# The first two tiles' expert products at the end of the causal stage, in shared PSUM banks

## Chip, cores and metric

One core of a Trainium2 chip. The metric is the device time in microseconds (us) of one execution of the whole program, the median over several runs; lower is better. The profile shows one execution, taken by the hardware profiler. Its engines: PE is TensorE's matmuls and PEld its weight loads, DVE is VectorE, ACT ScalarE, POOL GpSimd, SP SyncE; a name with a q (PEq) is the engine's instruction sequencer.

## The reference

Four residual blocks on x of shape (8, 512, 128), each `x = x + layernorm(block(layernorm(x)))`: a dilated attention, a ternary-weight linear layer, a 16-head attention with a gate, and a last block made of a causal grouped-query attention and a mixture of experts. Only the last one is touched:

```python
h = x + _gqa(_rmsnorm(x, attn_norm_w), wq, wk, wv, wo)     # causal, 16 heads of 8, 4 KV heads
out = h + _moe(_rmsnorm(h, ffn_norm_w), gate_w, expert_w)
# _moe, t: (tokens, 128)
logits = t @ gate_w.T                                      # 8 experts
w, sel = jax.lax.top_k(logits, 2)
w = jax.nn.softmax(w, axis=1)
comb = jnp.sum(w[..., None] * jax.nn.one_hot(sel, 8), axis=1)
for e in range(8):
    out = out + comb[:, e, None] * (t @ expert_w[e].T)
```

All eight experts' products are computed for every token, and weighted with `comb`, which is zero for six of them.

## The kernel before

The 4096 tokens are 32 tiles of 128 tokens, in four chunks of eight tiles (`TILES`, `CT`, `CHUNKS`). The program has five stages, one function each; every stage is a block in which each engine runs its own list of instructions, ordered against the others by semaphores alone. A stage ends with a barrier: each engine drains, GpSimd collects their signals and releases them, clears the stage's semaphores (`Phase.close`, line 55), and a second collect-and-release follows (recorded at lines 57 and 58).

**The causal stage** (`causal_attention_phase`, line 1287) works batch by batch in turns of three units for each pair of heads. TensorE makes transposed scores into `pT`, two PSUM buffers of two banks each (line 1320, used in turn); ScalarE takes their exponential into `P` and counts the semaphore `P` up (line 1566), 24 (`NT`) for each of the 8 (`B`) batches; GpSimd masks them (1446); TensorE multiplies them with the values into `pO` (1628) and transposes the result back to tokens (`by_token`, 1640, matmuls at 1643); ScalarE takes it out (`take`, 1546), VectorE inverts the sums (1482), GpSimd divides (1415). Score rings `pS` fill three further banks, `pO` the last one. After the last batch's scores nine more turns (`LAST_TURNS`) finish what is left of the outputs; their last TensorE work is the `by_token` of the last group.

In the last batch's turns, chunks 0 and 1 (`EARLY` = 2) of the mixture of experts are prepared as well (`early_turn`): attention by channel (transposes), projection, residual, h by channel, mean square, gate logits, the choice of two experts (`choose`, 1213) and the weights `comb` (`weigh`, 1238). So at the stage's end, `h` by channel of chunk 0 (`top.oT[0]`), and `comb` of chunks 0 and 1 are there.

**The experts stage** (`experts_phase`, line 1692) goes over turns u = 0 to 41, written out in each engine's list. In turn u:

- TensorE multiplies tile u's tokens (128 columns of `hT`) with all eight experts' weights, two matmuls of 512 columns in fp32 into `PE_[u % 3]`, a ring of three buffers of two banks each (lines 1943 to 1950). From tile 3 on it waits until VectorE has finished tile u - 3 (`scaled_d`). Each of these fp32 matmuls is two records in the profile, so a tile is four.
- ScalarE scales experts 0 to 3 out of PSUM into `T` (1907), once the product is there (`exp_psum`), and then VectorE adds experts 4 to 7, four fused multiply-adds (`scale_tile`, 1800 to 1808).
- GpSimd adds the four partial sums (1778, 1781).

The same lists hold the preparation of chunks 2 and 3, one step at a time, in the turns that `HEAD_AT` and the step tables set (lines 1724 to 1728): `HEAD_AT` is the turn of a chunk's first step, and each table gives the distance to it. TensorE's steps are the transposes into `PA` (recorded at line 1266), the projection (1275), the transposes of h (1266) and the gate (1282), at distances 0, 3, 6 and 9; VectorE's are residual (3), choose (8) and weigh (11); ScalarE's the copy (0), mean square (4), copy (6) and exponential (10). In a turn the tile comes first and the steps follow. The sum with h and the layernorm go by groups of four tiles: `total` of group g in turn 5 + 4g and `scalars` in turn 9 + 4g on VectorE, `normalise` in turn 11 + 4g on ScalarE, `finish` on GpSimd, and a store for each group.

Of the kernel before, what the change touches and what calls it, by code (L numbers as in the profile page):

```python
# [11 lines left out]
B, S, D = 8, 512, 128  # L12
R = 4
SEG = 64
TILES = B * R
CT = 8
# [6 lines left out]
HD4, KV4, NE = 8, 4, 8  # L23
# [1260 lines left out]
    last.then_inc(top.moe["logits"], 1)  # L1284


def causal_attention_phase(nc, top, dram):


# [9 lines left out]
    with ExitStack() as ctx:  # L1299
        ph = Phase(nc, ctx, "d_")  # L1300
        sm = ph.sems("part1 rest1 part2 rest2 parts mT_psum mT ST P masked PV O_sb O_T O_raw rden O_tok half_power")
        two = range(2)
        RING = 3
# [10 lines left out]
        P = [ph.sb(f"P{k}", [128, 2, PAIRW]) for k in range(4)]  # L1314
        OT = [ph.sb(f"OT{k}", [128, S]) for k in two]
        Or = [ph.sb(f"Or{k}", [128, QT, 2, 4, HD4 + 1]) for k in two]
        rden = [ph.sb(f"rden{k}", [128, QT, 2, 4]) for k in two]
        ring = ph.ps("pS", [128, RING, 512])
        pS = [ring[:, k, :] for k in range(RING)]
        pT = [ph.ps(f"pT{k}", [128, 2, 512]) for k in two]  # L1320
        pO = ph.ps("pO", [128, S])
        pM = [pT[ROWS_UNIT % 2][0:3 * HEADS, j, S - 128:S].bitcast(BF16) for j in two]

        NS, NT, NG = 3 * HEADS, 3 * HEADS // 2, KV4
# [56 lines left out]
        with nc.Block() as block:  # L1381
# [208 lines left out]
            def _(pe):  # L1590
# [75 lines left out]
                def early_turn(u):  # L1666
                    for step, k in early_steps(u, PE_STEPS):
                        if step == "attention_by_channel":
                            pe.wait_ge(S_max, B * NS)
                            pe.wait_ge(sm["O_tok"], 2 * (NG // 2) * (k + 1))  # L1670
                            wait(pe, early["hT"], k)
                            tokens_by_channel(nc, top, PA, O4[k]).then_inc(early["oT_psum"], 1)
                        if step == "project":
                            project(nc, pe, top, PA, k)
                        if step == "h_by_channel":
                            pe.wait_ge(early["h"], k + 1)
                            tokens_by_channel(nc, top, PA, h[k]).then_inc(early["hT_psum"], 1)
                        if step == "gate":
                            wait(pe, early["scale"], k)
                            gate(nc, pe, top, logits, k)  # L1680
# [5 lines left out]
                for pair, unit in LAST_TURNS:  # L1686
                    outputs(B, B // 2, 0, pair, unit)
                    early_turn(3 * HEADS // 2 + 3 * pair + unit)
        ph.close()


def experts_phase(nc, top, dram, out):
# [5 lines left out]
    with ExitStack() as ctx:  # L1698
        ph = Phase(nc, ctx, "e_")
# [3 lines left out]
        two = range(2)  # L1703
# [6 lines left out]
        st, mv = small("st", CT, 6), small("mv", CT, 2)  # L1710
        PART = NE // 2
        T = [ph.sb(f"T{k}", [128, PART, D]) for k in range(4)]
        PA = ph.ps("PA", [128, CT, D])
        RING = 3
        PE_ = [ph.ps(f"PE{k}", [128, NE, D]) for k in range(RING)]
        HALF = CT // 2
        GROUPS = TILES // HALF
        LAST = GROUPS - 1
# [2 lines left out]
        h = [top.N4[:, CT * c:CT * c + CT, :] for c in chunks]  # L1721
        O4 = [top.O4[:, CT * c:CT * c + CT, :] for c in chunks]

        HEAD_AT = {2: 1, 3: 12}
        PE_STEPS = {0: "attention_by_channel", 3: "project", 6: "h_by_channel", 9: "gate"}
        DVE_STEPS = {3: "residual", 8: "choose", 11: "weigh"}
        ACT_STEPS = {0: "attention_by_channel", 4: "mean_square", 6: "h_by_channel", 10: "exp_difference"}
# [13 lines left out]
        with nc.Block() as block:  # L1741
# [125 lines left out]
            @block.scalar  # L1867
            def _(act):
                def attention_by_channel(c):
                    act.wait_ge(early["oT_psum"], c + 1)  # L1870
                    nc.scalar.activation(oT[c][:, :, :], by_batch(PA[:, :, :]), ACT.Copy).then_inc(early["oT"], 1)

                def h_by_channel(c):
                    act.wait_ge(early["hT_psum"], c + 1)
                    nc.scalar.activation(hT[c][:, :, :], by_batch(PA[:, :, :]), ACT.Copy).then_inc(early["hT"], 1)

                def mean_square(c):
                    act.wait_ge(early["h"], c + 1)
                    for t in range(CT):

                        last = nc.scalar.activation(moe[c][:, t, :], h[c][:, t, :], ACT.Square,
                                                    accum_out=top.sq[c][:, t:t + 1])
                    last.then_inc(sm["sq"], 1)

                def deviation_last():

                    act.wait_ge(sm["mv"], LAST + 1)
                    nc.scalar.activation(by_group(std, LAST), by_group(mv, LAST)[:, :, 1], ACT.Sqrt, bias=top.eps[:, :])\
                        .then_inc(sm["dev"], 1)

                def normalise(g):
                    y, rstd, shift = by_group(h, g), by_group(rs, g), by_group(std, g)
                    act.wait_ge(sm["norm"], g + 1)
                    for t in range(2 if g == LAST else HALF):
                        last = nc.scalar.activation(y[:, t, :], y[:, t, :], ACT.Identity,
                                                    bias=shift[:, t:t + 1], scale=rstd[:, t:t + 1])
                    last.then_inc(sm["y"], 1)

                for u in TURNS:
                    if 0 <= u < TILES:  # L1900
                        act.wait_ge(early["comb"], u // CT + 1)
                        act.wait_ge(sm["exp_psum"], u + 1)
                        if u >= 4:

                            act.wait_ge(sm["summed"], u - 3)
                        for e in range(PART):
                            last = nc.scalar.activation(T[u % 4][:, e, :], PE_[u % RING][:, e, :], ACT.Copy,  # L1907
                                                        scale=comb[u // CT][:, u % CT, e:e + 1])
                        last.then_inc(sm["scaled_a"], 1)
                    for step, c in due(u, ACT_STEPS):  # L1910
                        if step == "attention_by_channel":
                            attention_by_channel(c)
                        if step == "h_by_channel":
                            h_by_channel(c)
                        if step == "mean_square":
                            mean_square(c)
                        if step == "exp_difference":
                            exp_difference(nc, act, top, c)
                            if c == CHUNKS - 1:
                                nc.scalar.activation(std[c][:, 0:1], top.eps[:, :], ACT.Sqrt)  # L1920
                    for g in group_due(u, "deviation"):
                        if g == LAST:
                            deviation_last()
                    for g in group_due(u, "normalise"):
                        normalise(g)

            @block.tensor
            def _(pe):
                def mm(out_, lhsT, rhs, start=True, stop=True):
                    return nc.tensor.matmul(out_, lhsT, rhs, start=start, stop=stop)  # L1930

                def attention_by_channel(c):
                    pe.wait_ge(early["scale"], c)
                    tokens_by_channel(nc, top, PA, O4[c]).then_inc(early["oT_psum"], 1)

                def h_by_channel(c):
                    pe.wait_ge(early["h"], c + 1)
                    tokens_by_channel(nc, top, PA, h[c]).then_inc(early["hT_psum"], 1)

                tokens = lambda c, t: hT[c][:, t // 4, 128 * (t % 4):128 * (t % 4) + 128]  # L1940

                for u in TURNS:
                    if 0 <= u < TILES:
                        if u >= RING:

                            pe.wait_ge(sm["scaled_d"], u - RING + 1)
                        for a in two:
                            last = mm(PE_[u % RING][:, 4 * a:4 * a + 4, :], tokens(u // CT, u % CT),
                                      top.gate_expT[:, NE + 512 * a:NE + 512 * a + 512])
                        last.then_inc(sm["exp_psum"], 1)  # L1950
                    for step, c in due(u, PE_STEPS):
                        if step == "attention_by_channel":
                            attention_by_channel(c)
                        if step == "project":
                            project(nc, pe, top, PA, c)
                        if step == "h_by_channel":
                            h_by_channel(c)
                        if step == "gate":
                            gate(nc, pe, top, PA[:, 0, :], c)
# [3 lines left out]
def sandwich(nc, dram, out):  # L1963
    with ExitStack() as ctx:
# [68 lines left out]
        dilated_and_ternary_phase(nc, top, dram)  # L2033
        gated_attention_phase(nc, top, dram)
        projection_phase(nc, top, dram)
        causal_attention_phase(nc, top, dram)
        experts_phase(nc, top, dram, out)


# [64 lines left out]
```

## Time and profile before

| | |
|---|---|
| median of 3 runs | 686.95 us (686.89 to 688.94) |
| profiled execution, its own time | 687.56 us |
| its span, first to last instruction | 685.8 us |
| mean granted TensorE clock | 0.84 of 2.4 GHz |
| busy: PE, DVE, ACT, POOL | 548.0, 506.5, 360.7, 268.0 us |
| causal stage's last work ends / experts stage's first matmul | 586.3 / 587.57 us after the span's start |

Times within the profile are counted from the span's start. An average busy share says little of one boundary between two stages; for this change the stretch from 584 us to the end of the span counts, and in it which wait ends last. The ends of matmuls are modelled, so the distance between starts tells more than a duration. A granted clock of 1.00 is 2.4 GHz, 0.50 is 1.2 GHz.

### The profile page before, as it was taken

Reading aid. Unit: us, or ns where it says so; the run is one execution under the profiler, and the core shown is the slowest. Engines: PE = TensorE matmul, PEld = TensorE weight load, DVE = VectorE, ACT = ScalarE, POOL = GpSimd, SP = SyncE. Lnnn points to the kernel's source line nnn. Section 1 sums busy time; section 2 is a strip of 40 time slices with the busy share of each in tenths; the row PEclk is TensorE's granted clock in tenths of the full one; section 3 lists DMA queues with packets and bytes.
Section 4 is the critical chain, followed back from the end, with each engine's and each line's share of the span. In section 5 each row is a group of like instructions: output and inputs, shape, how many; then the busy total and the mean of one; then the engine's idle time right before and its main releaser. Section 6 shows DMA issues by size and latency. Waiting matters only on the chain. (4 is left out here: it accounts for less than half of the span.)

```text
span 685.8 us, 11832 instructions
## 1 busy us (share of the span) xinstructions
PE 548.0 (80%) x3800; PEld 307.6 (45%) x3800; DVE 506.5 (74%) x2314; ACT 360.7 (53%) x738; POOL 268.0 (39%) x499
## 2 busy tenths in 40 slices
PE   1866478838967699867999999999999898798870
PEld 1856367727656466411233333333333454455420
DVE  6599999371273678688989999999997155269784
ACT  5841134500120467601478878878878754456762
POOL 2001007720002267810254544555455454266774
PEclk9996565555897699955599999999999998899996
DMA  8000000000000038510011211111210000000001
GB/s 315 1 1 1 0 1 1 0 1 0 1 1 1 0 119 227 169 62 6 1 36 32 63 31 35 34 33 37 58 36 1 7 1 1 2 0 16 32 16 61
DMA packets 17580, 24.77 MB, mean 36 GB/s; under 512 B 3246, under 2 KB 14014, under 8 KB 17342
## 3 DMA queue, kind: packets, MB, share of 16 engines
q1 hardware_dynamic: 16942, 21.91, 10.4%
q10 hardware_dynamic: 576, 2.10, 0.8%
q8 instruction: 30, 0.49, 0.3%
q14 instruction: 32, 0.26, 0.1%
HBM read 13.65 MB, written 10.35 MB: 35 GB/s over the span
## 5 line engine op out<-in xcount | busy, mean ns | idle before, releaser
L905 DVE CUSTOM_DVE_ANT_0 w_qkvT<-d_pS,w_qkvT 128x512 bf16<-128x512 f32 x480 | 203.9, 486 | 16.7 <-PE d_pS L896 11.8
L1566 ACT ACTIVATE d_P<-d_pT 128x768 f32<-128x768 f32 (+1 forms) x192 | 165.9, 882 | 62.7 <-PE d_pT L1592 61.1
L1446 POOL TENSOR_SCALAR_AFFINE_SELECT d_P<-d_P 128x256 f32<-128x256 f32 x256 | 102.6, 415 | 134.0 <-ACT d_P L1566 133.9
L896 PE MATMUL d_pS<-Ks,Qs 48*128 48x512 bf16 x480 | 97.8, 324 | 12.8 <-DVE hadamard L905 8.9
L1592 PE MATMUL d_pO<-d_P,V 128*32 128x512 f32 (+3 forms) x1024 | 98.5, 460 | 1.4 <-POOL d_P L1446 0.9
L1592 PE MATMUL d_pT<-Qs,Ks 51*128 51x512 bf16 (+3 forms) x512 | 72.9, 312 | 2.0 <-ACT d_mT L1536 2.0
L896 PEld LDWEIGHTS d_pS<-Ks,Qs 48*128 48x128 bf16 x480 | 32.2, 96 | 56.1 <-DVE hadamard L905 51.9
L1592 PEld LDWEIGHTS d_pT<-Qs,Ks 51*128 51x128 bf16 x512 | 20.7, 95 | 74.1 <-ACT d_P L1566 42.3
L1930 PE MATMUL e_PE<-gate_expT,w_qkvT 128*128 128x512 f32 x96 | 44.8, 614 | 6.3 <-DVE e_T L1804 3.5
L1804 DVE SCALAR_TENSOR_TENSOR e_T<-e_PE,comb,e_T 128x128 f32<-128x128 f32 x128 | 35.2, 343 | 19.2 <-ACT e_T L1907 19.2
L1907 ACT ACTIVATE e_T<-e_PE,comb 128x128 f32<-128x128 f32 x128 | 36.1, 377 | 24.8 <-issue 14.5
L905 DVE DVE_READ_ACCUMULATOR2_ANT hadamard<- 128x1 f32 x512 | 42.4, 83 | 0.0
L1592 PEld LDWEIGHTS d_pO<-d_P,V 128*32 128x32 f32 x1024 | 21.2, 110 | 32.6 <-issue 29.7
L1778 POOL TENSOR_TENSOR e_T<-e_T 128x256 f32<-128x256 f32 x32 | 24.4, 763 | 26.9 <-DVE e_T L1804 26.8
L453 POOL MEMSET a_expS<- 1x1024 f32 x4 | 3.8, 945 | 78.7 <-DVE a_q L263 78.7
L460 POOL TENSOR_SCALAR N<-X,a_mv_s,a_rs 128x128 f32<-128x128 f32 x32 | 25.1, 798 | 20.5 <-DVE a_rs L317 20.5
L1930 PEld LDWEIGHTS e_PE<-gate_expT,w_qkvT 128*128 128x128 f32 x96 | 18.0, 197 | 26.8 <-issue 21.1
L990 POOL MEMSET c_rms_bias<- 128x1 f32 x1 | 0.1, 98 | 76.3 <-POOLq L58 76.3
L978 POOL TENSOR_SCALAR N<-X,c_x_mv,c_rs 128x128 f32<-128x128 f32 x32 | 24.9, 783 | 7.3 <-DVE c_nb L1039 7.3
L1643 PE MATMUL d_pO<-ident,d_OT 128*128 128x128 f32 x128 | 21.7, 294 | 3.4 <-ACT d_OT L1554 3.1
L138 DVE BATCH_NORM_STATS2 a_st_s<-X 128x6 f32<-128x128 f32 x96 | 19.6, 278 | 6.1 <-DMA X<-in_x_dram 6.1
L368 ACT ACTIVATE a_nT<-a_PS 128x1024 f32<-128x1024 f32 x12 | 12.3, 1022 | 22.1 <-PE a_PS L476 22.0
(311 smaller groups left out, 1036.6 us busy)
## 6 DMA issues: line engine op xcount, KB each, us to landing
Qs<-q_stack SPq DMA_DIRECT2D x32, 192.0 KB, 3.1
q_stack<-Qp SPq DMA_DIRECT2D x8, 384.0 KB, 2.6
X<-in_x_dram ACTq DMA_DIRECT2D x4, 512.0 KB, 6.1
q_stack<-Qp SPq DMA_DIRECT2D x8, 256.0 KB, 2.5
out_dram<-e_moe SPq DMA_DIRECT2D x8, 256.0 KB, 2.0
w_qkvT<-in_w_qkvT_dram SPq DMA_DIRECT2D x1, 1536.0 KB
Ks<-k_stack SPq DMA_DIRECT2D x32, 48.0 KB, 3.2
q_stack<-Qp SPq DMA_DIRECT2D x8, 128.0 KB, 2.1
```

Source lines behind the costliest of these rows:

```text
L460: last = nc.gpsimd.tensor_scalar(n[c][:, t, :], X[c][:, t, :], mv["s3_"][c][:, t, 0:1], rs3[c][:, t:t + 1], ALU.subtract, ALU.mult)
L896: last = nc.tensor.matmul(dst[:, at:at + w], top.Qs[c][rows, h % 8, 128 * q:128 * q + 128], top.Ks[c][rows, h // 4 % 2, 0:w], start=True, ...
L905: last = nc.vector.tensor_tensor_reduce(out=junk[:, at:at + w], in0=src[:, at:at + w], in1=top.wide_mask[:, 512 - w:512], scale=1.0, scala ...
L978: last = nc.gpsimd.tensor_scalar(N4[:, R * n + t, :], X[:, R * n + t, :], x_mv[n][:, t, 0:1], rs[n][:, 0, t:t + 1], ALU.subtract, ALU.mult)
L1446: last = nc.gpsimd.affine_select(out=view, in_=view, compare_op=ALU.is_ge, fill=0.0, base=0, pattern=[[0, 2], [1, 128]], channel_multiplie ...
L1566: nc.scalar.activation(P[pair % 4][:, :, P_AT[unit]:P_AT[unit] + w], pT[(3 * pair + unit) % 2][:, :, 0:w], ACT.Exp, scale=float(HD4) ** -0 ...
L1592: return nc.tensor.matmul(out, lhsT, rhs, start=start, stop=stop)
L1643: last = nc.tensor.transpose(pO[:, 128 * q:128 * q + 128], OT[g % 2][:, 128 * q:128 * q + 128], top.ident[:, :])
L1778: nc.gpsimd.tensor_tensor(product[:, 0:2, :], product[:, 0:2, :], product[:, 2:4, :], ALU.add)\
L1804: last = nc.vector.scalar_tensor_tensor(out=T[u % 4][:, j, :], in0=PE_[u % RING][:, PART + j, :], scalar=comb[u // CT][:, u % CT, PART + j ...
L1907: last = nc.scalar.activation(T[u % 4][:, e, :], PE_[u % RING][:, e, :], ACT.Copy, scale=comb[u // CT][:, u % CT, e:e + 1])
L1930: return nc.tensor.matmul(out_, lhsT, rhs, start=start, stop=stop)
```

## The change

`pT` is taken from the causal stage and given to the top level, so that both stages hold the same four banks. At the very end of the causal stage's TensorE list, behind the last transposes, the products of tiles 0 and 1 are made into its two buffers. In the experts stage these are the first two buffers of the ring of three; TensorE starts with tile 2, ScalarE waits for no product in turns 0 and 1 (the barrier between the stages stands for it), and chunk 2's steps start in turn 2 instead of 1.

```diff
+EARLY_TILES = 2
+
+def expert_products(nc, top, dst, c, t):
+    tokens = top.oT[c][:, t // 4, 128 * (t % 4):128 * (t % 4) + 128]
+    for a in range(2):
+        last = nc.tensor.matmul(dst[:, a, :], tokens, top.gate_expT[:, NE + 512 * a:NE + 512 * a + 512], start=True, stop=True)
+    return last
...
 # causal_attention_phase
+        pT = top.pT
         ring = ph.ps("pS", [128, RING, 512])
         pS = [ring[:, k, :] for k in range(RING)]
-        pT = [ph.ps(f"pT{k}", [128, 2, 512]) for k in two]
...
                 for pair, unit in LAST_TURNS:
                     outputs(B, B // 2, 0, pair, unit)
                     early_turn(3 * HEADS // 2 + 3 * pair + unit)
+
+                pe.wait_ge(sm["P"], B * NT)
+                for t in range(EARLY_TILES):
+                    expert_products(nc, top, pT[t][:, :, :], 0, t)
         ph.close()
...
 # experts_phase
+        RING = 3
+        PE_ = [t[:, :, :].rearrange("p a (e d) -> p (a e) d", d=D) for t in (*top.pT, ph.ps("PE", [128, 2, 512]))]
         PA = ph.ps("PA", [128, CT, D])
-        RING = 3
-        PE_ = [ph.ps(f"PE{k}", [128, NE, D]) for k in range(RING)]
...
-        HEAD_AT = {2: 1, 3: 12}
+        HEAD_AT = {2: 2, 3: 12}
...
                         act.wait_ge(early["comb"], u // CT + 1)
-                        act.wait_ge(sm["exp_psum"], u + 1)
+                        if u >= EARLY_TILES:
+                            act.wait_ge(sm["exp_psum"], u - EARLY_TILES + 1)
...
-                    if 0 <= u < TILES:
+                    if EARLY_TILES <= u < TILES:
                         if u >= RING:
                             pe.wait_ge(sm["scaled_d"], u - RING + 1)
-                        for a in two:
-                            last = mm(PE_[u % RING][:, 4 * a:4 * a + 4, :], tokens(u // CT, u % CT),
-                                      top.gate_expT[:, NE + 512 * a:NE + 512 * a + 512])
-                        last.then_inc(sm["exp_psum"], 1)
+                        expert_products(nc, top, PE_[u % RING].rearrange("p (a e) d -> p a (e d)", a=2),
+                                        u // CT, u % CT).then_inc(sm["exp_psum"], 1)
...
 # sandwich
+        top.pT = [top.ps(f"pT{k}", [128, 2, 512]) for k in range(2)]
         causal_attention_phase(nc, top, dram)
```

## Rows read from the trace of the kernel before

**Rows 1.** The chain that ended last, in order of time: start us, us, what.

```profile
587.57 5.16 PE e_PE L1930 x8
592.73 0.87 PE e_PA L1266 x8
593.60 5.15 PE e_PE L1930 x12
598.75 3.61 PE e_PA L1275 x16
...
613.56 1.70 PE e_PA L1282 x16
...
630.50 4.39 PE e_PE L1930 x11
```

**Rows 2.** Timeline, causal stage's last work: start us, us, engine line op out<-in xcount.

```profile
584.12 0.66 PE L1643 MATMUL d_pO<-ident,d_OT 128*128 128x128 f32 x4 [0.71 <-ACT d_OT L1554]
584.81 0.36 ACT L1546 ACTIVATE d_Or<-d_pO 128x72 f32<-128x72 f32 x2 [0.75 <-PE d_pO L1643]
585.26 0.35 DVE L1482 RECIPROCAL d_rden<-d_Or 128x32 f32<-128x32 f32 x1 [4.59 <-ACT d_Or L1546]
585.70 0.63 POOL L1415 TENSOR_TENSOR O<-d_Or,d_rden 128x256 f32<-128x256 f32 x1 [6.95 <-DVE d_rden L1482]
```

**Rows 3.** Windows: length, busy us (x) PE PEld DVE ACT POOL, granted clock, DMA.

```profile
584.00:584.50 0.50, 0.38 (x3) 0.38 (x4) 0.00 (x0) 0.07 (x1) 0.00 (x0) 1.00 0.00 0
...
586.50:587.00 0.50, 0.00 (x0) 0.00 (x0) 0.00 (x0) 0.00 (x0) 0.00 (x0) 1.00 0.00 0
...
590.00:590.50 0.50, 0.50 (x2) 0.24 (x1) 0.00 (x0) 0.00 (x0) 0.00 (x0) 0.50 0.00 0
...
591.00:591.50 0.50, 0.50 (x3) 0.23 (x2) 0.00 (x0) 0.39 (x2) 0.00 (x0) 1.00 0.00 0
```

**Rows 4.** Semaphore events of the causal and projection stages' ends: ns, then start us.

```profile
L1381 PEldq DRAIN  x1: 700/700/700, 584.1 to 584.1; - x1
...
L1381 POOLq DRAIN  x1: 736/736/736, 585.7 to 585.7; - x1
...
L58 PEldq EVENT_SEMAPHORE  x1: 51/51/51, 587.5 to 587.5; - x1
...
L954 DVEq DRAIN  x1: 673/673/673, 304.3 to 304.3; - x1
...
L58 PEldq EVENT_SEMAPHORE  x1: 51/51/51, 305.7 to 305.7; - x1
```

**Rows 5.** Timeline, TensorE in the experts stage: behind tile 1, ahead of tile 13.

```profile
592.57 1.04 PE L1266 MATMUL e_PA<-ident,O 128*128 128x128 f32 x8
...
621.48 5.42 PE L1930 MATMUL e_PE<-gate_expT,w_qkvT 128*128 128x512 f32 x12 [1.82 <-DVE e_T L1804]
```

**Rows 6.** Timeline, ScalarE: tile 0, copy, tiles 5 and 6 (mean square between).

```profile
591.12 1.14 ACT L1907 ACTIVATE e_T<-e_PE,comb 128x128 f32<-128x128 f32 x4 [5.94 <-PE e_PE L1930]
...
593.85 1.04 ACT L1871 ACTIVATE w_qkvT<-e_PA 128x1024 f32<-128x1024 f32 x1
...
604.17 1.14 ACT L1907 ACTIVATE e_T<-e_PE,comb 128x128 f32<-128x128 f32 x4 [4.19 <-issue]
...
607.52 2.16 ACT L1907 ACTIVATE e_T<-e_PE,comb 128x128 f32<-128x128 f32 x8
```

**Rows 7.** Timeline, VectorE: choose, total, tiles 10 and 11, weigh, tile 13.

```profile
615.36 0.23 DVE L1218 TENSOR_TENSOR logit<-e_PA,rr 128x64 f32<-128x64 f32 x1 [1.13 <-PE e_PA L1282]
...
618.14 0.68 DVE L1813 TENSOR_TENSOR N<-N,e_moe 128x512 f32<-128x512 f32 x1
...
620.31 2.15 DVE L1804 SCALAR_TENSOR_TENSOR e_T<-e_PE,comb,e_T 128x128 f32<-128x128 f32 x8
...
624.16 0.16 DVE L1242 TENSOR_SCALAR weights<-weights 128x8 f32<-128x8 f32 x1
...
626.78 1.13 DVE L1804 SCALAR_TENSOR_TENSOR e_T<-e_PE,comb,e_T 128x128 f32<-128x128 f32 x4
```

## The prediction

> **What bounds the kernel now.** I read first the chain of waits, because only the stretch around the boundary between the causal and the experts stage is touched. It runs on TensorE from 587.57 us on: eight matmul records of the products of tiles 0 and 1 take 5.16 us, then transposes, products and projection follow back to back until the gate's matmuls, which start at 613.56 and take 1.70 [rows 1]. So from the stage's first instruction until about 615.3 TensorE sets the pace, and later the chain changes between VectorE, ScalarE and TensorE. The reader is to see there that one product tile is four records, 5.15 us for twelve, thus 1.72 us a tile at the steady rate, while the first two tiles took 592.57 - 587.57 = 5.0 us instead of 3.4 [rows 1, 5].
>
> Second, the timeline of the causal stage's last 3 us: TensorE's last four transposes start at 584.12 and follow each other so that it is free at about 584.8; ScalarE, VectorE and GpSimd then take the last group out (584.81, 585.26, 585.70) and TensorE has nothing until 587.57 [rows 2]. Third, the granted clock in half-microsecond windows: it is 1.00 (2.4 GHz) while those transposes run and still 1.00 at 586.5 to 587.0, where TensorE is idle; after that idle stretch it is 0.50 (1.2 GHz) under the first products, and 1.00 again from 591.0, after some 3 us of products [rows 3]. Fourth, the semaphore events of the stage's end: TensorE's drain ends at 584.8, GpSimd's at 585.7 + 0.74 = 586.4, and TensorE is released into the experts stage at 587.5, so 1.06 us behind the last drain; at the end of the projection stage the last drain (VectorE's) ended at 304.3 + 0.67 = 304.97 and the release came at 305.7, 0.73 us behind it [rows 4].
>
> **The edits, one by one.** *Products moved across the barrier.* Eight records leave the start of the experts stage (5.0 us there) and go behind the transposes. Their wait is for the last exponential, long past, so it costs nothing; nothing is queued behind them on TensorE but its drain, and the signal that ScalarE waits for comes ahead of them. They issue no DMA. They start at 584.8. If the clock stays at 2.4 GHz they take 8 x 0.43 = 3.44 us, to 588.2; if it falls for all of them, 8 x 0.86 = 6.86 us, to 591.6 (0.86 is twice 0.43, the clock being halved; before, low records followed by high ones made the 5.0). I take the first: the level was 1.00 at their start and stayed so until 587.0 with an idle engine [rows 3], and now the engine is busy in that stretch. As for the gap behind them (about 1 us), the clock stayed up through 1.82 us of idle ahead of tile 13, whose twelve records with their neighbours took 5.42 us as everywhere at the high rate [rows 5].
>
> The Trainium skill ("TensorE: Matmul & The Clock Gate", the part on the clock gate) says that the throttled clock is the default and that sustained activity releases it, which speaks against work put behind a thin stretch; by it the products could run at 1.2 GHz in part or in whole, and the sum would be that of the first rival.
>
> *The barrier.* It now waits for TensorE instead of GpSimd: it is the new wait that the change adds, and all four other engines stand behind it. 588.25, plus a handshake of between 0.73 and 1.06 (the two cases above [rows 4]); I take 0.85, because TensorE, like VectorE in the projection's end, comes last while GpSimd has long been drained. Release at 589.1, first matmul (tile 2) at 589.15, the 0.07 being that of before [rows 1, 4]. Before, TensorE had done tiles 0 and 1 at 592.57 and turned to the transposes [rows 5]. Gain at this point: 592.57 - 589.15 = 3.4 us.
>
> *ScalarE's missing waits.* Tiles 0 and 1 need no signal: ScalarE starts at 589.1 instead of 591.12 [rows 6], and VectorE one ScalarE tile later, at 590.3. Tile 3 reuses the first bank and needs VectorE's tile 0, done by about 591.4; TensorE comes to it at 591.74, so the ring of three has no new wait. The third ring buffer and the other banks change place, with no operation attached: nothing.
>
> *Chunk 2's steps one turn later.* Transposes, projection, h by channel and gate (0.87 + 3.61 + 0.87 + 1.70 = 7.05 us [rows 1]) keep their sizes. On TensorE ten tiles (2 to 11) now stand ahead of the gate's end instead of eleven: it ends at 589.15 + 10 x 1.717 + 7.05 = 613.4, where before it ended at 613.56 + 1.70 = 615.26. Then tile 12, the next transposes and tile 13 run to 613.4 + 1.72 + 0.87 + 1.72 = 617.7.
>
> What did VectorE make of it before? Between the gate and tile 10 it did choose (615.36 to 618.14), total and scalars (618.14 to 620.31), then tile 10, and TensorE sat idle for 1.82 us ahead of tile 13 [rows 5, 7]. After the change, total(1) and scalars(0) are still in turn 9 but choose is in turn 10, behind tile 10. ScalarE: tile 6's product ends at 602.2, tile and mean square take 607.52 - 604.17 = 3.35 us [rows 6], to 605.65; tiles 7 and 8 1.05 each, the copy 1.0 and tile 9 1.05: 609.8. VectorE: tile 9 until 610.95, total and scalars 2.25, tile 10 1.05, choose 2.8, tile 11 1.05: 618.1. Tile 14 needs that and starts at 618.15 instead of 617.7. The stall of 1.82 becomes 0.5, a gain of 1.3. Its bounds are a stall of nothing (gain 1.8) and the old one (gain 0).
>
> *What is late next.* VectorE, behind tile 13 (done at 620.2): weigh, at most 626.78 - 624.16 = 2.6, total and scalars 2.25, tile 14 1.05, makes 626.1. TensorE asks for tile 17 after tiles 14 to 16 and the projection, 618.15 + 5.15 + 3.61 = 626.9. So 0.8 us of cover are left. From turn 14 on both kernels do the same steps in the same order; the projection of chunk 3, tile 16 (630.50 before [rows 1]) and all that hangs on it come earlier by the whole gain.
>
> **The sum.** 3.4 + 1.3 = 4.7 us. The profiled execution took 687.56 us (span 685.8 and 1.76 around it): 682.9. The median of the runs, 686.95, is 0.6 below the profiled one, and this gives **682.3**.
>
> **The rivals.** *First, a low clock under the early products.* If the clock is down when they start and rises after some 3 us of them, as in the experts stage before [rows 3], they take 5.1 instead of 3.44 us, the gain is 1.7 smaller, 3.0: 684.0. For it: the level changes at moments that need not lie the same way to the work in every execution, and 3 us later, under the first products of before, it is down; against it: the transposes at 584.12 ran at 1.00. At the low level for all of them, the gain falls to 1.3: 685.7.
>
> *Second, the stall only moves.* If VectorE still makes TensorE wait 1.8 us around tiles 13 to 17, the start's 3.4 us is all: 683.6. For it: total, choose and weigh are as long as ever; against it: the cover worked out above.
>
> *Third, no difference.* VectorE's pile behind tile 13 exceeds its cover of 0.8 us by another 3 or more, so that most of the gain is returned at tile 17: about 685.5 to 686. For it: such VectorE operations stretch beside GpSimd ones (this weigh took 2.6 us); against it: it would have to double. The change does what it says, as far as the diff shows: the products do leave the stage.
>
> *Fourth, slower, by one mechanism: the clock stays low across the barrier.* All eight records at 0.86 put tile 2 at 584.8 + 6.86 + 0.9 = 592.56, and each further tile at the low level costs 1.72 more. With the 1.3 of the stall, two such tiles (low until 599.4) give 3.44 - 1.3 = +2.1 us, 689.1; from there on it is measurably slower. Against it: before, the clock came back by 591.0 after 3 us of just this work [rows 3].
>
> **How the numbers follow.** Forecast 0.58, first rival 0.17 (with its extreme), second 0.14, third 0.08, fourth 0.03. About 0.3%, 2.1 us, is what a measurement of this kernel can tell from no change. Faster by more: the forecast and the first two but for the extreme, 0.87; within: 0.10; slower: 0.03. The range takes in a full loss of the stall and the shorter handshake at its low end (4.7 + 0.5 + 0.1, and a little for the runs' own spread: 681.2) and both first rivals, to 685.2, at its high end; outside are the third and fourth and the first's extreme.
>
> **What would show it.** Right: eight product records from 584.8 to 588.2 (0.43 us apart) in the causal stage; the release 0.7 to 1.1 us behind TensorE's drain; ScalarE's tile 0 at about 589.1; the gate ending near 613.4; an idle of about 0.5 instead of 1.82 us ahead of tile 14 and little ahead of tile 13; tile 16 some 4.7 us earlier and the tail unchanged in length. Wrong: records 0.86 us apart (first or fourth rival); an idle of 1.5 us or more at tiles 13 to 17 released by VectorE (second, third); a release much later than 1.1 us behind the drain.

## The result and the profile after

The changed kernel took 683.59 us (median of 6 runs, 683.05 to 684.03), the kernel before 689.0 (6 runs, 686.89 to 690.23); the ratio of the two is 0.9925, with a 95% interval of 0.9908 to 0.9941. In a second comparison the ratio was 0.992 (0.9892 to 0.9948). That is 4 to 6 us faster in the first, around the 4.7 us that were forecast; 683.59 lies 1.3 us above the forecast 682.3 and within its range of 681.2 to 685.2. The three runs of the kernel before that were known at first, with a median of 686.95, were its quicker ones. All ratios here and below leave out two disturbed executions, one of 2357.49 us (of the version with one early tile) and one of 710.1 us (of the kernel before).

The profiled execution of the changed kernel took 683.05 us, its span is 681.3 us. TensorE's timeline of it, to be held against [rows 1, 2, 5]; columns are start us, us, engine, line, operation, tiles, shapes, count, idle before and releaser:

```profile
583.38 0.65 PE L1654 MATMUL d_pO<-ident,d_OT 128*128 128x128 f32 x4 [0.71 <-ACT d_OT L1565]
583.87 3.60 PE L1294 MATMUL pT<-gate_expT,w_qkvT 128*128 128x512 f32 x8
588.66 1.96 PE L1294 MATMUL e_PE<-gate_expT,w_qkvT 128*128 128x512 f32 x4 [1.19 <-PEq L58]
590.45 1.04 PE L1266 MATMUL e_PA<-ident,O 128*128 128x128 f32 x8
...
615.66 1.88 PE L1294 MATMUL pT<-gate_expT,w_qkvT 128*128 128x512 f32 x4
618.23 1.99 PE L1294 MATMUL e_PE<-gate_expT,w_qkvT 128*128 128x512 f32 x4 [0.69 <-DVE e_T L1819]
...
625.38 1.88 PE L1294 MATMUL pT<-gate_expT,w_qkvT 128*128 128x512 f32 x4
...
637.19 1.98 PE L1294 MATMUL pT<-gate_expT,w_qkvT 128*128 128x512 f32 x4 [1.68 <-DVE e_T L1819]
```

The rows are, from above: the last transposes of the causal stage, the eight early records, tile 2, the transposes of chunk 2, tile 13, tile 14, tile 16 and tile 21. The early products run right behind the transposes, 0.43 us apart, 3.6 us in all. Tile 2 starts at 588.66. The idle of 1.82 us ahead of tile 13 [rows 5] has gone, and tile 14 has one of 0.69.

The granted clock of the changed kernel, in windows as in [rows 3]:

```profile
584.50:585.00 0.50, 0.50 (x2) 0.19 (x1) 0.35 (x1) 0.00 (x0) 0.05 (x1) 1.00 0.00 0
...
588.00:588.50 0.50, 0.00 (x0) 0.00 (x0) 0.00 (x0) 0.00 (x0) 0.00 (x0) 1.00 0.00 0
...
589.50:590.00 0.50, 0.50 (x2) 0.19 (x1) 0.19 (x1) 0.50 (x4) 0.00 (x0) 1.00 0.05 16
```

It stays at 2.4 GHz through the products, the idle 1.19 us of the barrier, and the first tiles behind it, where the kernel before had 1.2 GHz.

The events of the stage's end, to be held against [rows 4]:

```profile
L1392 PEldq DRAIN  x1: 4053/4053/4053, 583.4 to 583.4; - x1
...
L1392 POOLq DRAIN  x1: 737/737/737, 584.9 to 584.9; - x1
...
L58 PEldq EVENT_SEMAPHORE  x1: 51/51/51, 588.5 to 588.5; - x1
```

These are TensorE's drain, GpSimd's drain and TensorE's release. TensorE's drain now ends last, at 583.4 + 4.05 = 587.45, 1.8 us behind GpSimd's (585.6), and the release follows 1.05 us behind it.

**A measure that is free of the earlier stages.** The work ahead of the last transposes is the same in every kernel here (at most PSUM banks change place), yet they start anywhere from 579.5 to 585.2 us in the profiled executions, so a good part of the spread between executions arises before anything that was edited. So the kernels are compared below by the stretch *behind the start of the last transposes*, each number being a start in TensorE's timeline less that start (584.12 before, 583.38 changed), and the last column the rest of the span (span less that start, so good to 0.05 us).

| kernel | TensorE done with tile 1, or at the work behind it | tile 16 | tile 21 | span's end |
|---|---|---|---|---|
| before | 8.45 | 46.22 | 57.54 | 101.7 |
| before, second profile | 8.38 | 46.16 | 58.61 | 102.8 |
| changed | 5.28 | 42.00 | 53.81 | 97.9 |
| changed, second profile | 5.28 | 41.99 | 53.80 | 98.0 |

The start brings 8.45 - 5.28 = 3.2 us, by tile 16 it is 4.2, by tile 21 3.7, and 3.8 remain at the end (101.7 - 97.9); against the second profile of the kernel before it is 4.8. From tile 21 to the end all four take 44.1 to 44.2 us, so nothing changes there. These second profiles come from the experiments.

### The profile page after: what moved, and what is told of

Same layout as the page of the kernel before. It is cut to its first block and busy times, and to the rows that moved or that the text cites. A ratio compares the mean times of both kernels' runs of the same rounds, so it can differ in the third digit from the quotient of the medians.

```text
span 681.3 us, 11830 instructions
## 1 busy us (share of the span) xinstructions
PE 548.2 (80%) x3800; PEld 308.0 (45%) x3800; DVE 507.4 (74%) x2314; ACT 360.6 (53%) x738; POOL 267.5 (39%) x499
## 5 line engine op out<-in xcount | busy, mean ns | idle before, releaser
L1577 ACT ACTIVATE d_P<-pT 128x768 f32<-128x768 f32 (+1 forms) x192 | 165.9, 882 | 63.2 <-PE pT L1603 61.6
L1603 PE MATMUL d_pO<-d_P,V 128*32 128x512 f32 (+3 forms) x1024 | 99.9, 466 | 1.4 <-POOL d_P L1457 0.9
L1603 PE MATMUL pT<-Qs,Ks 51*128 51x512 bf16 (+3 forms) x512 | 72.7, 312 | 2.0 <-ACT d_mT L1547 2.0
L1603 PEld LDWEIGHTS pT<-Qs,Ks 51*128 51x128 bf16 x512 | 20.8, 95 | 75.0 <-ACT d_P L1577 43.7
L1923 ACT ACTIVATE e_T<-pT,comb 128x128 f32<-128x128 f32 x88 | 24.9, 375 | 18.2 <-issue 11.3
L1819 DVE SCALAR_TENSOR_TENSOR e_T<-pT,comb,e_T 128x128 f32<-128x128 f32 x88 | 24.2, 341 | 11.9 <-ACT e_T L1923 11.9
L1294 PE MATMUL pT<-gate_expT,w_qkvT 128*128 128x512 f32 x64 | 29.7, 597 | 1.7 <-DVE e_T L1819 1.7
L476 PE MATMUL a_PS<-ident,X 128*128 128x128 f32 x64 | 13.9, 389 | 9.8 <-DVE X L296 6.1
```

The costliest lines, as they stand in the source:

```text
L1294: last = nc.tensor.matmul(dst[:, a, :], tokens, top.gate_expT[:, NE + 512 * a:NE + 512 * a + 512], start=True, stop=True)
L1577: nc.scalar.activation(P[pair % 4][:, :, P_AT[unit]:P_AT[unit] + w], pT[(3 * pair + unit) % 2][:, :, 0:w], ACT.Exp, scale=float(HD4) ** -0 ...
L1603: return nc.tensor.matmul(out, lhsT, rhs, start=start, stop=stop)
L1819: last = nc.vector.scalar_tensor_tensor(out=T[u % 4][:, j, :], in0=PE_[u % RING][:, PART + j, :], scalar=comb[u // CT][:, u % CT, PART + j ...
```

## Experiments

The theory to be tested: the gain has two sources, the start (early products, themselves in two parts, work moved under the barrier and a clock that is kept up) and the turn of chunk 2's steps; and part of it is given back between tiles 16 and 21, where VectorE's weigh meets a GpSimd operation. Rivals: one source only; a stall that only moves; a favoured comparison.

### The turn alone

```diff
 # in the kernel before
-        HEAD_AT = {2: 1, 3: 12}
+        HEAD_AT = {2: 2, 3: 12}
```

> The kernel before with chunk 2's steps one turn later and nothing else. My theory: the experts stage starts as before (tiles 0 and 1 take 5.0 us), but choose no longer stands with total and scalars ahead of one tile, so the 1.82 us that TensorE idles ahead of tile 13 goes and VectorE's pile behind tile 13 gives back some 0.5 us: 1.1 to 1.4 us faster than the kernel before. Rival (the turn only pays together with the early products, because only a TensorE that runs ahead meets VectorE there): within 0.4 us of the kernel before.

Ratio to the kernel before 0.9974 (0.9947 to 1.0002), 1.8 us faster at the middle, with an interval that just takes in no change. The trace is sharper, but its execution had the low clock for longer. Its windows:

```profile
593.50:594.00 0.50, 0.50 (x2) 0.33 (x1) 0.50 (x3) 0.00 (x0) 0.00 (x0) 0.50 0.00 0
...
594.50:595.00 0.50, 0.50 (x2) 0.21 (x2) 0.00 (x0) 0.00 (x0) 0.44 (x1) 1.00 0.00 0
```

Products began at 588.33 and the clock rose only at about 594, so that three tiles took 596.48 - 588.33 = 8.15 us instead of 5.0 + 1.72 = 6.72, thus 1.4 more. Less that 1.4, tile 16 comes at 46.54 - 1.43 = 45.1 (before: 46.2), so the turn is worth 1.1 us there, and tile 21 at 56.9 (57.5 before): 0.6 is left, half being given back. The stretch to the end is 102.5, or 101.1 less the 1.4: 0.6 better than the first profile of the kernel before. The idle fell from 1.82 to 0.70, as in the changed kernel. The rival that the turn only pays together with the early products has fallen for the stretch up to tile 16; and since the same half microsecond is given back here without any early product, it belongs to the turn and not to the earlier start.

### The early products alone

```diff
 # in the changed kernel
-        HEAD_AT = {2: 2, 3: 12}
+        HEAD_AT = {2: 1, 3: 12}
```

> The changed kernel with chunk 2's steps back in turn 1. My theory: tile 2 starts some 5.3 us behind the last transposes' start as in the changed kernel, TensorE's idle ahead of tile 13 is back to 1.8 us, and the total gain against the kernel before is the start's alone, 3.2 us, so 1.0 us or a little more slower than the changed kernel. Rival (the turn brings nothing by itself, VectorE's wait only moves from tile to tile): as fast as the changed kernel within 0.3 us.

Ratio 0.9923 (0.9898 to 0.9948), which cannot be told from the changed kernel's by the runs. In the trace the work behind tile 1 starts at 5.29 as expected, and the idle is back:

```profile
616.14 1.04 PE L1266 MATMUL e_PA<-ident,O 128*128 128x128 f32 x8
619.00 1.98 PE L1294 MATMUL pT<-gate_expT,w_qkvT 128*128 128x512 f32 x4 [1.82 <-DVE e_T L1819]
```

Tile 16 comes at 43.09: 3.1 us better than before, 1.1 worse than the changed kernel. So up to tile 16 the parts add: 3.1 + 1.1 = 4.2. The end is 99.7, 1.8 worse than the changed kernel instead of 1.0: tile 21 came only at 55.56. The loss between tiles 16 and 21 is thus not the same in every kernel. The trace has a reason at hand: chunk 2's weigh takes 3.8 us here (621.67 to 625.46), with its first operation at 0.71 us and its last at 1.20, against 2.6 us in the first profile of the kernel before. The second profile of the kernel before, below, has the same outcome.

### Early products made and thrown away

```diff
 # in the kernel before, at the end of the causal stage's TensorE list
+                pe.wait_ge(sm["P"], B * NT)
+                for t in two:
+                    for a in two:
+                        mm(pT[t][:, a, :], top.oT[0][:, 0, 128 * t:128 * t + 128],
+                           top.gate_expT[:, NE + 512 * a:NE + 512 * a + 512])
```

> The kernel before with the same eight product records at the end of the causal stage, whose results nobody reads: tiles 0 and 1 are made again in the experts stage. It separates the clock from the moved work. If the early records keep the clock at 2.4 GHz, the second making takes 3.4 instead of 5.0 us, and the barrier is 1.0 to 1.1 us later: 0.5 us faster than before to 0.2 slower, with tiles 0 and 1 together at 3.4 us; then 1.6 us of the start's gain is the clock's. Rival (the clock has nothing to do with it): tiles 0 and 1 take 5.0 us again, and the kernel is 1.0 to 1.2 us slower than before.

Ratio 0.9993 (0.9968 to 1.0018). TensorE's timeline:

```profile
584.80 3.60 PE L1592 MATMUL d_pT<-gate_expT,w_qkvT 128*128 128x512 f32 x8
589.59 3.67 PE L1936 MATMUL e_PE<-gate_expT,w_qkvT 128*128 128x512 f32 x8 [1.19 <-PEq L58]
593.10 1.04 PE L1266 MATMUL e_PA<-ident,O 128*128 128x128 f32 x8
```

and a window under its first tile, with the granted clock at 1.00:

```profile
589.50:590.00 0.50, 0.41 (x1) 0.30 (x2) 0.00 (x0) 0.00 (x0) 0.00 (x0) 1.00 0.04 16
```

The second making takes 593.10 - 589.59 = 3.5 us instead of 5.0, though the barrier is 1.8 us later (5.29 instead of 3.45): tile 1 is done at 8.80 instead of 8.45, and the span's end is 102.1. Extra work that nobody reads costs 0.35 us only, as the second making now runs at 2.4 GHz. The rival (5.0 us again, 1.0 to 1.2 us slower) has fallen. My band ended at 0.2 us slower; the barrier's cost was taken at 1.0 to 1.1 and was 1.8. Of the start's 3.2 us, 5.0 - 3.5 = 1.5 are the clock's, and the rest is work that no longer stands behind the barrier (3.5) less the later barrier (1.8).

### One early tile instead of two

```diff
-EARLY_TILES = 2
+EARLY_TILES = 1
```

> The changed kernel with one early tile instead of two: tile 0 ahead of the barrier, tile 1 behind it. My theory: TensorE's drain ends ahead of GpSimd's division, so the barrier comes some 1.0 us earlier than in the changed kernel and as early as in the kernel before; tile 1 then takes 1.7 us behind it, so tile 2 starts 0.6 to 0.8 us later than in the changed kernel, and the time is 0 to 0.8 us above it: of two early tiles the second is paid back by the later barrier in part. Rival (the clock falls in the 2 us of idle between tile 0 and tile 1): tile 1 takes 3.4 us and the time is 1.7 to 2.5 us above the changed kernel's.

Ratio 0.9926 (0.9896 to 0.9956). Its TensorE timeline:

```profile
583.56 1.88 PE L1294 MATMUL pT<-gate_expT,w_qkvT 128*128 128x512 f32 x4
586.64 1.96 PE L1294 MATMUL pT<-gate_expT,w_qkvT 128*128 128x512 f32 x4 [1.19 <-PEq L58]
588.43 1.88 PE L1294 MATMUL e_PE<-gate_expT,w_qkvT 128*128 128x512 f32 x4
```

The clock stayed up through the idle between tile 0 and tile 1 (tile 1 took 1.79 us). The barrier is as early as in the kernel before (tile 1 starts at 3.57), tile 2 starts at 5.36 instead of 5.28, tile 16 at 42.01 and the end is 97.9: the second early tile is worth 0.1 us. What it takes from behind the barrier it adds in front of it. With one early tile TensorE's drain (583.1 + 2.38 = 585.5) and GpSimd's (584.6 + 0.74 = 585.3) end nearly together; with the second, TensorE's is the last one by 1.8 us. (I had expected 0.6 to 0.8 us: the release plus 1.8 us already gives 5.4.)

### The two kernels once more

The changed kernel and the kernel before, unaltered.

> The changed kernel once more, beside the next one and in the same rounds. My theory of the parts: 3.2 us from the start, 1.1 from the turn, 0.5 given back where weigh meets GpSimd, so 3.8 us behind the last transposes, and more in executions in which the kernel before has the low clock for longer than its profiled one (one such showed 8.15 us for three tiles instead of 6.7): a median gain of 4 to 6 us. In the trace: records of the early products 0.43 us apart, weigh of chunk 2 over 2.5 us long where a GpSimd operation runs beside it. Rival (the first comparison was favoured by the earlier stages): 2.5 to 3.8 us.

> The kernel before once more, for its profile. My theory: the work behind the last transposes is the same, and only the time at the low clock at the start of the experts stage differs, as the clock's changes fall differently: tiles 0 and 1 take between 5.0 and 6.9 us, and from there on the same 93 us. Rival (other parts of the stage vary as well): the stretch behind tile 1 differs by over 0.5 us too.

The changed kernel: ratio 0.992 (0.9892 to 0.9948), 3.6 to 7.4 us, and the same stretches to 0.1 us as in its first profile. The kernel before: behind tile 1 everything is as in its first profile up to tile 16, and tile 21 is 1.07 us later, so my theory that only the clock's part varies has fallen. VectorE and GpSimd in this second profile, around chunk 2's weigh:

```profile
624.27 0.73 POOL L1778 TENSOR_TENSOR e_T<-e_T 128x256 f32<-128x256 f32 x1
624.31 0.72 DVE L1242 TENSOR_SCALAR weights<-weights 128x8 f32<-128x8 f32 x1
...
625.59 0.65 DVE L1248 TENSOR_TENSOR weights<-weights 128x8 f32<-128x8 f32 x1
...
626.71 1.26 POOL L1754 TENSOR_TENSOR e_moe<-N,X 128x512 f32<-128x512 f32 x1
626.87 1.19 DVE L1254 TENSOR_TENSOR comb<-pick 128x64 f32<-128x64 f32 x1
628.10 1.13 DVE L1804 SCALAR_TENSOR_TENSOR e_T<-e_PE,comb,e_T 128x128 f32<-128x128 f32 x4
```

weigh takes 628.10 - 624.31 = 3.8 us, against 2.6 in the first profile [rows 7]. Its last operation started 0.16 us behind GpSimd's 1.26 us sum of four tiles and ended just behind it; in the first profile it started ahead of it and took 0.49. But the two profiles part already at weigh's first operation, which took 0.72 us here and 0.16 there. GpSimd's operation beside it in the first profile:

```profile
624.12 0.78 POOL L1778 TENSOR_TENSOR e_T<-e_T 128x256 f32<-128x256 f32 x1
```

In both profiles GpSimd's start is on record 0.04 us ahead of VectorE's (624.12 and 624.16, 624.27 and 624.31), so the starts do not tell why one outcome or the other comes up. The same list of instructions has two outcomes here, 1.1 us apart. Of the five profiles with chunk 2's steps in turn 1, two have the short first operation (the first one of the kernel before, and the thrown-away products) and three the long one (this one, the early products alone, and the kernel before with the later sum, further down). The median of the runs does not tell them apart: with a usual start of the last transposes (584.2) and 1.8 us around the span, the first outcome gives 687.7 and the second 688.8, and 35 runs of the kernel before had a median of 688.35.

In the changed kernel's weigh another operation is caught:

```profile
620.16 0.16 DVE L1242 TENSOR_SCALAR weights<-weights 128x8 f32<-128x8 f32 x1
...
620.70 1.27 POOL L1769 TENSOR_TENSOR e_moe<-N,X 128x512 f32<-128x512 f32 x1
620.80 1.19 DVE L1248 TENSOR_TENSOR weights<-weights 128x8 f32<-128x8 f32 x1
...
623.37 0.69 DVE L1828 TENSOR_TENSOR N<-N,e_moe 128x512 f32<-128x512 f32 x1
```

Eight elements for each partition take 1.19 us, and weigh 3.2 us. On this the Trainium skill ("SBUF — State Buffer", the section on the two separate sides) has a rule: VectorE and GpSimd share a pair of ports which whoever starts first holds for the whole instruction, and a VectorE operation with two inputs in SBUF, or in a mode that uses both ports, waits for a GpSimd one (with two inputs, for one that reads SBUF). By that rule, the trace agrees for the two operations of 1.19 us: they have two such inputs, start 0.1 to 0.2 us behind the GpSimd sum and end with it. The one of 0.72 us has a single input and ends with GpSimd's of 0.73; whether it runs in such a mode no run here shows.

### GpSimd's sum cut small beside weigh

```diff
 # in the changed kernel, finish(g) on GpSimd
-                    nc.gpsimd.tensor_tensor(by_group(moe, g), by_group(h, g), by_group(X, g), ALU.add)\
+                    some = (lambda t: t[:, 0:1, 0:8]) if g == 0 else (lambda t: t)
+                    nc.gpsimd.tensor_tensor(some(by_group(moe, g)), some(by_group(h, g)), some(by_group(X, g)), ALU.add)\
```

> The changed kernel with GpSimd's finish of the first group of four tiles cut to 8 of its 512 elements for each partition; the rest of that group's last sum is left out, all other groups are whole. It takes the 1.27 us GpSimd operation away from beside chunk 2's weigh and moves nothing else. My theory: no operation of that weigh takes over 0.7 us, weigh takes 2.0 to 2.6 us instead of 3.2, the mean square of chunk 3 does not wait for VectorE's residual, and the stretch behind the last transposes is 97.3 to 97.6 us instead of 97.9. Rival (what is given back between tiles 16 and 21 has another cause): weigh is shorter but the stretch stays at 97.8 to 98.0 us. Other rival: weigh is as long as before, because the next GpSimd operation takes the place.

This kernel leaves out most of the last sum of the first four tiles, so its output is incomplete: it is a probe and no candidate. Ratio 0.9933 (0.991 to 0.9956); the stretch is 97.5 us instead of 97.9 and 98.0. The same two engines:

```profile
621.43 0.16 DVE L1242 TENSOR_SCALAR weights<-weights 128x8 f32<-128x8 f32 x1
...
621.97 0.20 POOL L1770 TENSOR_TENSOR e_moe<-N,X 128x8 f32<-128x8 f32 x1
622.07 0.17 DVE L1248 TENSOR_TENSOR weights<-weights 128x8 f32<-128x8 f32 x1
...
622.15 0.79 DVE L1250 TENSOR_TENSOR pick<-pick,weights 128x64 f32<-128x64 f32 x1
...
623.76 0.69 DVE L1829 TENSOR_TENSOR N<-N,e_moe 128x512 f32<-128x512 f32 x1
```

With the GpSimd operation at 0.20 us, VectorE's product is back at 0.17, and weigh takes 623.76 - 621.43 = 2.3 us. (One operation reached 0.79, a little over my 0.7, beside GpSimd's next one.) Tile 16 comes at 42.00 as in the changed kernel, tile 21 at 53.33 instead of 53.81. That is 11.3 us from tile 16 to tile 21, as in the first profile of the kernel before (57.54 - 46.22), where the changed kernel has 11.8. So nearly all of the half microsecond that was given back is this meeting of two engines. How it reaches tile 21 is in ScalarE's timeline of the changed kernel: the mean square of chunk 3 waited there for VectorE's residual, which stands behind weigh:

```profile
627.35 1.14 ACT L1923 ACTIVATE e_T<-pT,comb 128x128 f32<-128x128 f32 x4
628.85 0.31 ACT L1896 ACTIVATE e_moe<-N 128x128 f32<-128x128 f32 x1 [0.36 <-DVE N L1812]
```

With the sum cut small it starts right behind the tile ahead of it, without a wait:

```profile
628.61 1.14 ACT L1924 ACTIVATE e_T<-pT,comb 128x128 f32<-128x128 f32 x4 [0.92 <-issue]
629.63 0.33 ACT L1897 ACTIVATE e_moe<-N 128x128 f32<-128x128 f32 x1
```

### GpSimd's sum one turn later

```diff
-        GROUP_TURNS = {"total": 5, "deviation": 7, "scalars": 9, "normalise": 11, "finish": 13}
+        GROUP_TURNS = {"total": 5, "deviation": 7, "scalars": 9, "normalise": 11, "finish": 14}
```

This was tried in the changed kernel, in the kernel before, and with one early tile.

> The changed kernel with GpSimd's finish (the 1.27 us sum of four tiles) one turn later, 14 + 4g instead of 13 + 4g. My theory: chunk 2's weigh took 3.2 us in the changed kernel because its 8-element product started while that GpSimd operation ran and ended with it (1.19 us instead of 0.17); with it out of the way weigh takes 2.1 to 2.6 us, VectorE is 0.6 to 1.1 us earlier at tile 14, tile 21 comes 0.3 to 0.6 us earlier, and the kernel is 0.3 to 0.6 us faster behind the last transposes (97.3 to 97.6 us instead of 97.9). Rival (weigh is slow for another reason, or another GpSimd operation takes the place): within 0.15 us.

> The same edit in the kernel before, whose two profiles differ by 1.1 us behind the last transposes (101.68 and 102.77), with weigh at 2.6 and 3.8 us. My theory: the slow case, in which weigh's last operation falls under GpSimd's 1.27 us one, does not come up any more: 101.1 to 101.8 us, and the median 0.5 to 1.1 us under the kernel before's. Rival: 102.8 us again, no difference in the median.

> One early tile and the later finish together, a candidate for the fastest version. My theory: the second early tile is worth nothing (97.93 against 97.92 us), the later finish is worth 0.3 to 0.6, so 97.3 to 97.6 us behind the last transposes, a median 0.3 to 0.6 us under the changed kernel's, which these rounds may not tell from no difference. Rival: 97.9 us.

All three went the other way: ratios 0.9966 (0.9944 to 0.9988), 1.0033 (1.0006 to 1.0059) and 0.9965 (0.9944 to 0.9986), thus 2 to 3 us slower each than without the edit, and stretches of 102.0, 105.4 and 100.6 us. In the kernel before, weigh did lose its 1.26 us neighbour: its last operation took 0.23 us, but its first one 0.71, and weigh 2.8. In the changed kernel the meeting only moved within weigh: the sum started at 621.87 and now caught the last operation, which took 1.20 us from 622.02, and weigh took 3.1 us instead of the 2.1 to 2.6 expected; with one early tile it was the same. And the sum now meets VectorE's `scalars` in later groups; in the changed kernel with the later sum:

```profile
635.03 1.26 POOL L1769 TENSOR_TENSOR e_moe<-N,X 128x512 f32<-128x512 f32 x1
635.19 1.12 DVE L1844 SCALAR_TENSOR_TENSOR e_std<-e_mv,e_rs 128x4 f32<-128x4 f32 x1
...
648.56 1.26 POOL L1769 TENSOR_TENSOR e_moe<-N,X 128x512 f32<-128x512 f32 x1
648.72 1.12 DVE L1844 SCALAR_TENSOR_TENSOR e_std<-e_mv,e_rs 128x4 f32<-128x4 f32 x1
```

An operation on four elements takes 1.12 us, and this one has tiles and TensorE behind it: the idle ahead of tile 21 is 2.20 us instead of 1.68. In the first of the three the clock also fell twice behind such longer stalls (tile 21's four records take 3.66 us instead of 1.98), in the other two once. One turn for all groups did not dodge the meetings; other offsets were not tried.

### Chunk 2's steps yet another turn later

```diff
-        HEAD_AT = {2: 2, 3: 12}
+        HEAD_AT = {2: 3, 3: 12}
```

It was run with two early tiles and with one.

> The changed kernel with chunk 2's steps another turn later (3 instead of 2): weigh is in turn 14, away from total(2) and scalars(1) in turn 13, choose in turn 11, and the gate behind tile 12. My theory (VectorE's order around tiles 13 to 17 sets what is given back): the 0.5 us between tile 16 and tile 21 is kept, but TensorE now has the gate behind tile 12 and the transposes of chunk 3 directly behind it wait for choose: within 0.7 us of the changed kernel, tile 21 up to 0.5 us earlier. Rival (each turn of delay brings what the first one brought): 1 us faster than the changed kernel. Other rival (the gate is too late, VectorE stands idle for it): 1 us slower.

> One early tile and turn 3 together, the candidate for the fastest version: if one early tile is worth what two are (as the stretch behind the last transposes showed, 97.93 against 97.92 us) and the later turn costs nothing, it is within 0.5 us of the changed kernel; if the later turn keeps what weigh gives back, 0.5 us faster. Rival: the gate behind tile 12 makes VectorE wait, 1 us slower.

Ratios 0.9936 (0.9911 to 0.9962) and 0.9938 (0.9912 to 0.9965): about 1 us behind the changed kernel, though the intervals overlap. The stretches are 99.4 and 99.6 us. With one early tile, tile 16 comes at 41.56, 0.4 us earlier than in the changed kernel, so up to there the turn itself did no harm. Tile 21 comes at 53.96, 0.15 us later than in the changed kernel, behind VectorE's `total`, which took 1.72 us instead of 0.68 beside GpSimd's sum. And both profiled executions lost TensorE's clock within the stage. With two:

```profile
615.87 1.09 PE L1266 MATMUL e_PA<-ident,O 128*128 128x128 f32 x8 [0.39 <-DVE logit L1218]
616.80 3.38 PE L1294 MATMUL pT<-gate_expT,w_qkvT 128*128 128x512 f32 x4
```

Tile 13's four records take 3.2 us to tile 14's start instead of 1.7, right behind the gate's narrow matmuls and the transposes: 1.5 us. With one early tile the same happens at tile 21, behind an idle of 2.25 us. Other executions may well keep it: of the twelve with one early tile, three took 680.8 to 680.9 us at a mean granted clock of 0.848, the profiled one 685.3 at 0.839. That mean is over the whole program, so it does not say in which stage they differ.

**No version beat the changed kernel** by more than can be measured. One early tile equals it.

## Why the prediction was right, point by point

- *What bounds it, and the forecast itself.* The mechanism is right, and the forecast of 4.7 lies in the first interval, 4.1 to 6.3 us. But part of that is luck. The 4.7 was worked out from the first profile of the kernel before, and against that one the gain is 3.8 us behind the last transposes: 0.2 less from the barrier, 0.2 less from the turn, 0.5 given back. Against the second profile it is 4.8, as weigh there takes 1.2 us more; and an execution with the low clock for longer, as in the one with the turn alone (1.4 us), would gain more still. The forecast counted neither of the two.
- *Products at 2.4 GHz.* Right: 3.6 us, from the moment at which the transposes end. The first rival (low clock) has not come up in any of the ten profiles with early records. Throwing the products away showed that the clock is 1.5 of the 3.2 us.
- *Barrier.* TensorE is last, as said, but the term was mis-sized: 1.05 us instead of the 0.85 taken, which is the upper one of the two bounds [rows 4]. The reason given for the lower value, that GpSimd has drained long before, is not borne out: it had drained 1.8 us before, and the release took as long as in the kernel before. The 0.3 us more than at the projection stage's end lie in the first of the two barriers, where GpSimd's two signals are 0.4 us apart (587.5 and 587.9) and there 0.1 (305.0 and 305.1); why is open. The start's gain was 3.2 instead of 3.4.
- *The turn.* Right: the idle of 1.82 became 0.69 (forecast 0.5), worth 1.1 instead of 1.3, and the turn alone gave the same 1.1 in the kernel before.
- *"What is late next" and "come earlier by the whole gain".* This is the one step that failed. The cover of 0.8 us was worked out for TensorE's wait at tile 17. The work that was late is another: residual, then ScalarE's mean square, then tile 17 on ScalarE. And "weigh, at most 2.6" was no bound: it took 3.2 us here, 3.8 in the kernel before's second profile. It gave back 0.5 us.
- *The second rival* (the stall only moves) is in part true by that: 0.5 of 1.1. *The third* named the mechanism that did it, VectorE operations stretched beside GpSimd ones, but priced it at 3 us or more, and it was 0.6 for weigh. The fourth did not happen.
- *The sum against the median.* The three runs known then were among the quick ones of a kernel whose later median is 688.4; so the predicted time came out 1.3 us low, though the difference lay within the interval.
- *Two small slips in the working* carry nothing. The starts of [rows 1] are those of the chain and lie 0.16 us behind the timeline's (gate 613.56 and 613.40), so before, the gate ended at 615.10 and not at 615.26. And 602.2 + 3.35 is 605.55, not 605.65.

What stays open: why the last transposes start up to 5.7 us apart between executions, ahead of all that was edited, and how often each outcome of weigh comes up and what decides it; five profiles, two one way and three the other, are too few to say.

## What to carry to other kernels

In this kernel, work that an engine can do while the others finish a stage was worth what it took off behind the barrier, only until that engine's own drain became the last one; beyond that, more of it was worth nothing (the second tile). On TensorE it paid twice, since with matmuls in the gap the granted clock stayed at 2.4 GHz into the next stage, so that even discarded ones were nearly free. Where two times are compared, look for an earlier stretch that varies by itself, and count from behind it. Before moving a step by a turn, look on VectorE at which other steps stand in that turn, and on GpSimd at what runs beside them.

## What the runs showed of the hardware that was not expected

- A VectorE operation on 4, 8 or 64 elements for each partition took 1.12 to 1.20 us instead of 0.13 to 0.23 when it started 0.1 to 0.2 us behind a GpSimd sum of 1.26 us, and ended with it. The same program's stretch was 101.7 or 102.8 us, by how such meetings fell out; the starts on record do not tell which way they will.
- The two barriers and the clearing of semaphores at this place took about 1.05 us from the last drain to TensorE's release, whichever engine came last (0.73 us at the projection stage's end).
- Between the stage's start and its idle tail, the granted clock fell to 1.2 GHz in every profile whose idle ahead of tile 21 was 2.2 us (right there in two of the four, 12 to 13 us later, behind another idle of 2.2 us, in the other two), and in none where it was 1.7 us, but for the kernel with the gate behind tile 12 and two early tiles, where it fell at tile 13.
